# Last local attention layer: query features read from PSUM, and the sums of the second end unit in two halves

## What is computed

```python
def _L3_attn_ref(x, w_qkvw, w_out):
    H, G, DIM = 16, 4, 128
    HD = DIM // H // G                       # 2
    B, S, dim = x.shape                      # 64, 32, 128
    qkvw = x @ w_qkvw                        # 512 columns
    chunks = jnp.split(qkvw, G, axis=-1)
    subs = [jnp.split(t, G, axis=-1) for t in chunks]
    q, k, v, w = (jnp.concatenate([subs[i][n] for i in range(4)], axis=0) for n in range(4))
    def shp(t):
        return t.reshape(B * G, H, -1, HD).swapaxes(1, 2)
    q, k, v = (shp(q), shp(k), shp(v))
    w = w.reshape(B * G, H, -1, HD)
    attn = jax.nn.softmax(q @ k.swapaxes(-2, -1) * HD ** (-0.5), axis=-1)
    o = (attn @ v).swapaxes(1, 2).reshape(B, S, dim)
    return o * w.reshape(B, S, dim) @ w_out
```

## Time and profile before

| | |
|---|---|
| median of three runs | 2057.41 us |
| the profiled execution, on the device | 2055.21 us |
| its span | 2053.4 us |
| PE busy | 1747.0 us, 85% |
| DVE busy | 1340.8 us, 65% |
| ACT busy | 1045.8 us, 51% |
| GpSimd (POOL) busy | 904.9 us, 44% |
| chain that ended last, by engine | PE 55%, DVE 20%, issue 9%, ACT 7%, DMA 4%, POOL 4% |

### The profile page before, as it was taken

How to read it: one execution, slowest core, us unless ns; L and a number is a source line. 1 busy time by engine, 2 the same in 40 slices (tenths; PEclk the granted TensorE clock), 3 DMA queues, 4 the chain that set the end, 5 groups by cost and what they waited for, 6 DMA issues and landing times.

```text
span 2053.4 us, 50642 instructions
## 1 busy us (share of the span) xinstructions
PE 1747.0 (85%) x20238; PEld 1177.5 (57%) x20238; DVE 1340.8 (65%) x3578; ACT 1045.8 (51%) x2709; POOL 904.9 (44%) x1088
## 2 busy tenths in 40 slices
PE   7678999999988789998888879999999997447596
PEld 4323556566664555654566656776676764125496
DVE  6799996576675565455672277656877876666622
ACT  4445665487873652224532346666666753115243
POOL 2343554555551523320514152326767578433543
PEclk9878999999999999999978999999999998766598
DMA  9000000100008100034014301000000000040197
GB/s 362 1 1 0 0 1 1 77 5 5 4 5 348 67 4 0 1 153 197 3 68 133 110 22 42 22 22 20 13 25 19 11 12 1 10 155 30 57 308 231
DMA packets 60429, 130.68 MB, mean 64 GB/s; under 512 B 16714, under 2 KB 38941, under 8 KB 54561
## 3 DMA queue, kind: packets, MB, share of 16 engines
q1 hardware_dynamic: 56896, 121.32, 16.5%
q0 software_dynamic: 3296, 6.12, 0.9%
HBM read 107.97 MB, written 20.12 MB: 62 GB/s over the span
## 4 chain that ended last, share of the span: by engine, by line
PE 55%; DVE 20%; issue 9%; ACT 7%; DMA 4%; POOL 4%; SPq 1%; POOLq 1%; DVEq 0%; ACTq 0%
PE PS L3321 4%; PE PS L2516 4%; PE PS L424 3%; PE PS L3368 3%; PE PS L3353 2%; PE PS L3352 2%; DMA arena<-in_ctx 2%; PE PS L3310 2%; PE PS L460 2%; PE PS L1521 2%; PE PS L2316 2%; PE PS L4328 2%; PE PS L4319 2%; PE PS L1497 2%; PE PS L1082 1%
## 5 line engine op out<-in xcount | busy, mean ns | idle before, releaser
L321 POOL TENSOR_TENSOR arena<-arena 128x4 f32<-128x4 f32 (+3 forms) x109 | 118.7, 1089 | 347.4 <-DVE arena L264 225.9
L1655 POOL TENSOR_TENSOR arena<-arena 128x128 f32<-128x128 f32 x448 | 164.4, 404 | 53.0 <-PE PS L1703 15.6
L3436 ACT ACTIVATE arena<-PS,arena 128x289 f32<-128x289 f32 x256 | 127.6, 503 | 73.2 <-DVE arena L3550 72.8
L3550 DVE TENSOR_REDUCE arena<-PS 128x1 f32<-128x289 f32 x256 | 113.5, 454 | 71.9 <-PE PS L3321 67.8
L3321 PE MATMUL PS<-arena 128*128 128x289 f32 x512 | 150.6, 417 | 10.4 <-ACT arena L3436 7.5
L1258 POOL TENSOR_TENSOR arena<-arena 128x512 f32<-128x512 f32 x64 | 83.9, 1311 | 109.8 <-DVE arena L1403 109.8
L1610 ACT COPY arena<-PS 32x128 f32<-32x128 f32 x384 | 99.5, 259 | 21.8 <-PE PS L1511 17.7
L3321 PEld LDWEIGHTS PS<-arena 128*128 128x128 f32 x512 | 87.4, 191 | 34.5 <-ACT arena L3436 16.8
L3279 POOL TENSOR_TENSOR arena<-arena 128x1024 f32<-128x1024 f32 x14 | 33.0, 2355 | 159.8 <-ACT arena L3427 159.8
L3564 DVE TENSOR_TENSOR arena<-PS,arena 128x580 f32<-128x580 f32 x128 | 97.6, 762 | 4.4
L368 PE MATMUL PS<-arena 128*128 128x512 f32 x166 | 89.9, 677 | 9.5 <-DVEq L4635 8.7
(11 more groups left out here) (471 smaller groups left out, 4768.6 us busy)
## 6 DMA issues: line engine op xcount, KB each, us to landing
arena<-in_ctx SPq DMA_DIRECT2D x32, 1091.0 KB, 10.2
arena<-in_f_w SPq DMA_DIRECT2D x39, 514.0 KB, 5.5
arena<-in_ctx SPq DMA_DIRECT2D x16, 834.0 KB, 16.3
lists<-arena SPq DMA_DIRECT2D x8, 1040.0 KB, 10.8
arena<-in_f_w SPq DMA_DIRECT2D x32, 256.0 KB, 2.9
arena<-in_ctx SPq DMA_DIRECT2D x16, 512.0 KB, 3.9
arena<-in_mid SPq DMA_DIRECT2D x1, 3796.5 KB, 12.4
arena<-in_late SPq DMA_DIRECT2D x1, 3204.0 KB, 11.4
```

What stands on the lines that cost most here:

```text
L321: e.tensor_tensor(x, x, half.broadcast_to(list(x.shape)), ALU.pow).then_inc(*T.done("norm_root", tag))
L1655: k = e.tensor_tensor(dst[:, b], spread(src[:, b, :], [P, HG, S], 1), spread(self.g.C["headmask"], [P, HG, S], 2), ALU.mult)
L3436: e.activation(self.weights(n, k, 0, UL), PS[:, self.score_bank(n, k), 0:UL], ACT.Exp, bias=self.st[:, h, k:k + 1], accum_out=self.st[:, h ...
L3550: e.tensor_reduce(self.st[:, n % 2, k:k + 1], PS[:, self.score_bank(n, k), 0:UL], AXX, ALU.max, negate=True).then_inc(*T.done("k3_least", ...
```

## The change

- DVE's product reads its query feature from PSUM banks 4 to 7, where PE made it, and not from the copy in SBUF.
- GpSimd's order: both products come right after weigh 10, ahead of weigh_more 10 and the passes of unit 11.
- DVE's order: both products come first, then the residuals of quarters 0 and 1 without their statistics, which are now separate (`begin`), then the rest in a new order. The rows of quarters 0 to 2 come ahead of the last residual.
- PE sums unit 0 and the first two banks of unit 1 before the subtraction of unit 0, and the other two banks behind it.
- Unit 1 is weighted by GpSimd alone, in two passes, so ACT's second exponential and DVE's `weigh` for unit 1 are left out.
- `mix_dve` waits for the total of its unit.

```diff
+    def feature_of(self, z, r, f, lo, n):
+        return z.rearrange("p h (r j e) -> p r e j h", r=4, e=2)[:, r, f, lo:lo + n, :]
+
     def feature(self, q, r, f, lo, n):
-
-        return self.z[q % 2].rearrange("p h (r j e) -> p r e j h", r=4, e=2)[:, r, f, lo:lo + n, :]
+        return self.feature_of(self.z[q % 2], r, f, lo, n)
...
-        def add_products(u):
-            for n, b in enumerate(range(4 * u, 4 * u + 4)):
+        def add_products(u, which):
+            for n in which:
+                b = 4 * u + n
                 for w in T.due(free[b], ("m3_first", ("end", u)), ("m3_second_dve", ("end", u))):
                     e.wait_ge(*w)
...
-            m.then_inc(*T.done("m3_scores", u))
+            m.then_inc(*T.done("m3_scores", (u, which[-1])))
...
-        add_products(0)
+        add_products(0, range(4))
+        add_products(1, range(2))
         subtract(0)
-        add_products(1)
+        add_products(1, range(2, 4))
         subtract(1)
...
-            e.activation(banks, banks, ACT.Exp, scale=float(2 ** -0.5)).then_inc(*T.done("m3_exp_again", u))
+            if u == 0:
+                e.activation(banks, banks, ACT.Exp, scale=float(2 ** -0.5)).then_inc(*T.done("m3_exp_again", u))
...
         def weighed(u):
             for w in T.due(("m3_exp", ("end", u))):
                 e.wait_ge(*w)
-            e.tensor_tensor(self.by_four(self.vp[u][:, 0, :]), self.ex[u].rearrange("p j (h g) -> p j h g", g=self.NP),
-                            spread(self.at_end(u, 2, 0), self.wide_end, 2), ALU.mult).then_inc(*T.done("m3_weighed", ("end", u)))
+            for f in range(1 + u):
+                m = e.tensor_tensor(self.by_four(self.vp[u][:, f, :]), self.ex[u].rearrange("p j (h g) -> p j h g", g=self.NP),
+                                    spread(self.at_end(u, 2, f), self.wide_end, 2), ALU.mult)
+            m.then_inc(*T.done("m3_weighed", ("end", u)))
 
         self.root_pool(e, T, NT - 1)
-        for what, U in rest[:-2]:
+        for what, U in rest[:2]:
             self.pass_pool(e, T, what, U)
         products(0)
-        for what, U in rest[-2:]:
+        products(1)
+        for what, U in rest[2:]:
             self.pass_pool(e, T, what, U)
-        products(1)
         weighed(0)
         weighed(1)
...
         total, mixed = self.total[:, u, :], sums.rearrange("p (e r) -> p e r", e=2)
+        for w in T.due(("m3_total", U)):
+            e.wait_ge(*w)
         e.reciprocal(total, total).then_inc(*T.step())
...
         def products(u):
+            made = PS[:, 4:8, :].rearrange("p b (a d) -> p (b a) d", a=4)
             for w in T.due(*features):
                 e.wait_ge(*w)
-            e.tensor_tensor(self.pb[u].rearrange("p j (h g) -> p j h g", g=NP), spread(self.at_end(u, 0, 1), self.wide_end, 3),
+            e.tensor_tensor(self.pb[u].rearrange("p j (h g) -> p j h g", g=NP),
+                            spread(self.feature_of(made, 0, 1, JE * u, JE), self.wide_end, 3),
                             spread(self.at_end(u, 1, 1), self.wide_end, 2), ALU.mult).then_inc(*T.done("m3_second_dve", ("end", u)))
...
-        def weigh(u):
+        def whole(u):
             total = self.total_end[:, u]
...
             e.reciprocal(total, total).then_inc(*T.step())
+
+        def weigh(u):
             for w in T.due(("m3_exp_again", u)):
                 e.wait_ge(*w)
...
             e.tensor_tensor(x, four(PS[:, b, :]), x, ALU.add).then_inc(*T.done("m3_added", q))
+
+        def begin(q):
             for w in T.due(("m3_added", q)):
                 e.wait_ge(*w)
             self.after.begin_dve(e, T, q)
...
         products(0)
-        for q in range(2):
-            residual(q, q)
         products(1)
+        residual(0, 0)
+        residual(1, 1)
         self.mix_dve(e, T, mixes[0], self.mixed)
+        begin(0)
+        self.total_dve(e, T, totals[1])
         maxima(0)
-        self.total_dve(e, T, totals[1])
+        begin(1)
+        self.mix_dve(e, T, mixes[1], self.mixed)
+        whole(0)
         maxima(1)
-        self.mix_dve(e, T, mixes[1], self.mixed)
         weigh(0)
-        weigh(1)
         mix(0)
+        whole(1)
         mix(1)
-        for q in range(2, NQ):
-            residual(q, q - 2)
-            self.after.begin_rows_dve(e, T, q - 2)
-        self.after.begin_rows_dve(e, T, NQ - 2)
+        residual(2, 0)
+        begin(2)
+        for q in range(NQ - 1):
+            self.after.begin_rows_dve(e, T, q)
+        residual(3, 1)
+        begin(3)
```

More of the change, by code:

```diff
@@ L4044, in maxima @@
             rows = PS[:, 4 * u:4 * u + 4, :].rearrange("p b (r g) -> p (b r) g", g=NP)
-            for w in T.due(("m3_scores", u)):
+            for w in T.due(("m3_scores", (u, 3))):
                 e.wait_ge(*w)
             e.tensor_reduce(self.least_end[:, u], rows, AXX, ALU.max, negate=True).then_inc(*T.done("m3_least", ("end", u)))
-        def weigh(u):
+        def whole(u):
             total = self.total_end[:, u]
```

## The result

The changed kernel took 2036.56 us (median of seven runs, 2028.25 to 2041.51), and the kernel before 2051.82 us in runs beside it (seven, 2048.52 to 2058.58). The ratio is 0.9905, with a 95% interval of 0.9889 to 0.9921: 19.5 us less, between 16.2 and 22.8. The ratio is not the quotient of the medians: these lie 15.3 us apart, and the means 17.8 us. So the gain of the whole kernel is known to some 15 to 23 us and no better. The forecast was 17.6 us less and 2039.8 us, with a range of 2033 to 2049. Both lie within that; how much of the agreement is luck is said further down. On a second chip the same pair of kernels gave 2054.75 and 2074.41 us, a ratio of 0.9895 (0.9870 to 0.9921).

A forecast was written before the change was run, and what follows sets the result against it. The prediction took one serial chain of waits between engines in the layer's tail as the bound, with a 16.54 us DVE hole; 12.7 us (last mixed row) + 4.9 (last rows) = 17.6, so 2057.4 became 2039.8 us, range 2033 to 2049.

The forecast's parts named there:

- the path: Chain of waits from the products through both units to the last mixed row: 1791.5 in place of 1804.24, 12.7 us gained.
- the rival of the collision: DVE's and GpSimd's products still alternate despite the PSUM operand: 6.8 us later, gain 10.8, 2046.6 us; chance 0.08.
- the sum: 12.7 us up to the last mixed row plus 4.9 us from hiding the last rows: 17.6 us gained.
- the lock: DVE operation with two SBUF inputs excludes GpSimd ones reading SBUF; could add up to 2.9 us at mixing unit 10.
- one wait of L267 (1.3 us): In unit 0's statistics, tiny L267 comes at about 1750 and waits for GpSimd's weighing of unit 11 to 1751.3.
- The slow and the fast subtraction: PE's subtraction 0 after about 2.5 us idle takes 3.7 us; subtraction 1 after 3.8 us idle takes 6.3; chance 0.45.
- both fast: Rival: both PE subtractions run at the fast clock, gain 2.6 us more, 2037.2 us; chance 0.15.
- both slow: Rival: both PE subtractions run at the slow clock, gain 2.6 us less, 2042.4 us; chance 0.17.
- The cover of 2.1 us for each product: DVE's 4.2 us wait ahead of mixing unit 10 lets each PSUM-fed product cost 2.1 us more before it shows.
- The next layer's clock: Rival: PE's attention heads turn slower, up to 23.7 us lost, 2063.5 us; chance 0.12 for part, 0.03 for all.

The follow-up runs named there:

- the kernel with two edits: Changed kernel with DVE weighing unit 1 from PSUM again and GpSimd's weigh_more 10 ahead of its products: first product to last rows 72.70 us (changed: 77.43), ratio 0.9885.

## Why the prediction held, and where it didn't

The time, the gain and the path came out as forecast, and the step that failed is the one on the cause: "The gain is the order on GpSimd's and DVE's queues, not the halves." The runs showed in its place that GpSimd's order alone gains nothing (95.22 us against 95.14), that 7.4 of the 17.7 us hang on the operand in PSUM, which this sentence leaves out (though the rival of the collision prices it at 6.8), and that one part of the change, GpSimd's weighing of unit 1, costs 3.5 us: the path priced GpSimd's two passes and never compared them with DVE's one.

The time of 2039.8 us was hit in part by luck. It started from a median of 2057.41 us, of three runs; seven runs gave 2051.82. Less 17.6 this is 2034.2, and 2036.56 was measured: the base was 5.6 us too high, and the medians lie 2.3 us less far apart than the sum says.

Step by step, in us from the start of DVE's first product:

| step | predicted | measured |
|---|---|---|
| DVE's product from PSUM | 3.5 | 3.7 |
| GpSimd's second product ends | 9.7 | 9.8 |
| DVE's wait ahead of mixing 10, with the reciprocal in it | 4.2 | 4.1 |
| maxima 0 start | 20.4 | 20.23 |
| subtraction 0 | 3.7 | 3.71 |
| maxima 1 start | 31.5 | 31.41 |
| subtraction 1 | 6.3 | 6.26 |
| DVE's wait ahead of the last reduction | 7.2 | 6.99 |
| last mixed row | 58.7 | 58.48 |
| from it to the last sums | 14.1 | 14.15 |
| from these to the last rows | 4.7 | 4.80 |

The first maxima came 1.3 us earlier (21.50 to 20.23) where 1.2 was the forecast; L267 waited for GpSimd there and took 1.58 us in place of 0.17, as it had taken 2.82 at 1738.83. It has one tensor input, so these rows don't fit the prediction's condition of two SBUF inputs on either side: a `TENSOR_SCALAR` waits as well. The price of the PSUM operand came from L4060, which was the nearest row; at 3.67 us it equals the undisturbed SBUF product of 3.68, so that row would have been as good a guide. The short multiplications of unit 10, for which the lock would have added up to 2.9 us, had all begun when GpSimd's next pass did, at 1752.48 (they ran from 1751.78 to 1752.57): they missed it narrowly. In the kernel with two edits the first of them met a pass and took 0.68 us in place of 0.29.

**What was wrong in it.** None of these moved the sum by much.

- *The halves.* I held that they brought nothing. Undone, they cost 0.7 us in either way. With the sums behind, PE is idle for 5.51 us ahead of subtraction 0, not 2.23, and it takes 5.19 us, not 3.71. But 0.7 us is within what one subtraction scatters, so this is open.
- *The queues' order as the cause.* This is the step named above. The operand in PSUM is worth 7.4 us within the change and 3.9 without the rest, so the parts are not a sum but hang on each other. I had costed the collision for the two products and one wait of L267 (1.3 us), not for all the tiny operations of the statistics, which took 10.2 us in one kernel.
- *The slow and the fast subtraction read from the gap ahead of them.* It came out as read, but the rule isn't one. Behind gaps of 2.1 to 2.4 us the eight passes were fast nine times (3.71) and slow once (5.40). Behind gaps of 3.3 to 5.9 us they took 5.1 to 6.4. Even the same gap of 3.99 us gave 5.40 in some kernels and 6.26 to 6.43 in others. So that the forecast of 3.7 and 6.3 was met to 0.1 us is luck by up to 1 us. What the prediction takes from the Trainium skill stands in TensorE: Matmul & The Clock Gate under Why this matters for your kernels, and taken for every gap it doesn't hold here: the nine fast subtractions speak against it. The chances that I gave to both fast or both slow were right to be there: the clock moved the tail of several experiments by 1 to 2 us from what I expected.
- *The cover of 2.1 us for each product.* It holds for DVE alone. A slower first product also delays PE's sums, which the prediction itself gives only 2.5 us to spare. 3.7 us more moved subtraction 0 by 1.2 us, and only the clock won this back, so that 0.1 was left: the small cost is luck.
- *What the sum leaves out.* It took the time up to the tail and behind it as fixed. DVE's first product starts anywhere from 1726.85 to 1745.35 us in the fourteen traces, and the changed kernel alone has 1736.81 and 1745.35. The sum is right for the tail, but single executions scatter by more than all of it, and only the ratio over many runs shows it.

The rival of the collision that stays (6.8 us of the gain lost) describes the kernel with the SBUF operand well: 7.4. The next layer's clock gave nothing back in the profiled execution: from the last rows to that layer's first expert weights (SP's L4213) it was 117.3 us before and 116.8 after (L4233 there).

## What to carry to other kernels

When two engines hold each other up, look at the tiny operations too: three of 0.17 us cost 10.2 us because each met a long pass of the other engine. For long passes, feeding one operand from PSUM frees both. For the tiny ones only another place was tried: where GpSimd is idle, those of quarter 1 take 0.17 us each in the changed kernel. Before a pass is moved to a less busy engine, compare when that engine's result would be there with when the old one would have made it: here GpSimd was only 44% busy and still ended the unit 3.5 us later.

## What the runs showed of the hardware

- Two passes of 128x2048 on DVE and GpSimd with two SBUF inputs each don't share but alternate: 16.57 us for two on each engine, which take 9.8 us side by side when DVE has one operand in PSUM.
- In the kernel with GpSimd's order alone, a DVE operation on four elements a partition waited up to 4.4 us for a GpSimd pass, and `TENSOR_SCALAR` (one tensor input, in SBUF) waited 2.6 us there, so it is held up as well as `TENSOR_TENSOR`.
- Behind the same gap of 2.39 us in one execution, eight equal matmuls took 5.40 us once (granted clock 0.50 from 1754.5 to 1757.5) and 3.71 us once.
- The stretch from the last rows to the next layer's first expert weights took 116.2 to 117.3 us in the first pair of traces and in the four taken on one chip, and 125.0 to 128.5 us in the eight taken on three other chips, whatever the kernel. I didn't find out why; a ratio is only good with both kernels on one chip.
